# One expert tile normalised and stored a step, and TensorE two tiles ahead instead of one

## What is computed

```python
x = layernorm(x + attention(x))      # x: 4 x 1024 tokens of 128; 16 heads, 32 random features a head
# attention: q, k, v = x @ w_qkv;  elu1 features of q and k;  linear attention;  @ w_out + b_out
scores = x @ wr + br                 # router, 8 experts, the best one for each token
h = gelu(x @ w1[e] + b1[e])          # 128 -> 512, e the token's expert
y = h @ w2[e] + b2[e]                # 512 -> 128
out = layernorm(x + y)
```

## Time and profile before

| what | us |
|---|---|
| median of 3 runs (216.15 to 216.47) | 216.17 |
| span of the profiled execution, first to last instruction | 241.8 |
| PE busy in that span | 203.7 |
| DVE, ACT, POOL busy | 158.7, 146.5, 126.4 |

### The profile page before, as it was taken

The page is one execution under the profiler, slowest core; times in us unless marked ns, Lnnn a source line. Parts: engine busy times, 40 slices in busy tenths (PEclk is TensorE's granted clock), DMA queues, the critical chain, the costliest instruction groups (busy, mean ns, idle before and its releaser), DMA issues.

```text
span 241.8 us, 5983 instructions
## 1 busy us (share of the span) xinstructions
PE 203.7 (84%) x1717; PEld 160.5 (66%) x1717; DVE 158.7 (66%) x563; ACT 146.5 (61%) x379; POOL 126.4 (52%) x162
## 2 busy tenths in 40 slices
PE   7989999999999999998888359994997886999800
PEld 2768888888645555544357358993996875999700
DVE  1577686876669999999967226772664463467640
ACT  3488888888576887766275326662474453565810
POOL 8334252525971086665736761078553844577470
PEclk9999999999999999999999959999799998899965
DMA  4999999999710000012763334665564564461000
GB/s 114 246 395 409 412 409 411 412 408 321 225 52 0 5 34 34 34 36 54 237 163 117 94 101 114 169 188 157 144 178 130 164 186 138 134 184 45 11 28 0
DMA packets 28416, 40.45 MB, mean 167 GB/s; under 512 B 3497, under 2 KB 18126, under 8 KB 28384
## 3 DMA queue, kind: packets, MB, share of 16 engines
q1 hardware_dynamic: 26112, 35.80, 45.5%
q0 software_dynamic: 2272, 4.27, 5.2%
HBM read 17.95 MB, written 22.56 MB: 168 GB/s over the span
## 4 chain that ended last, share of the span: by engine, by line
PE 49%; issue 13%; POOL 11%; another core or an unknown queue 10%; ACT 8%; DVE 4%; DMA 1%; ACTq 1%; POOLq 1%; DVEq 0%
PE pair L312 13%; PE pair L792 13%; PE pair L805 7%; POOL sorted_rows L533 6%; PE bank L645 5%; ACT qfeat L964 3%; PE pair L785 2%; POOL rstd L514 2%; POOL out_dram L552 2%; PE bank L805 2%; PE pair L615 1%; PE bank L625 1%; ACT x L932 1%; DMA wqkv_sb<-in_L_attn_w_qkv_dram 1%
## 5 line engine op out<-in xcount | busy, mean ns | idle before, releaser
L964 ACT ACTIVATE qfeat<-pair,w_sb 128x128 f32<-128x128 f32 x156 | 44.6, 368 | 30.3 <-PE pair L792 17.5
L792 PE MATMUL pair<-xsT,w_slot 128*128 128x128 f32 x312 | 44.9, 290 | 4.3 <-ACT xsT L954 2.6
L792 PEld LDWEIGHTS pair<-xsT,w_slot 128*128 128x128 f32 x312 | 40.2, 202 | 6.7 <-issue 3.3
L533 POOL DMA_INDIRECT sorted_rows<-x,dest x32 | 31.6, 986 | 12.4 <-issue 8.8
L312 PE MATMUL pair<-wkv_part,xT_all 128*128 128x256 f32 x192 | 33.9, 321 | 1.1 <-ACT vals L886 0.8
L805 PE MATMUL pair<-w_sb,qfeat 128*128 x232 | 33.1, 289 | 0.7 <-issue 0.7
L561 POOL TENSOR_TENSOR ksum<-kfeat 128x512 f32<-128x512 f32 x12 | 16.6, 1379 | 30.7 <-DVE kfeat L1049 30.7
L805 PEld LDWEIGHTS pair<-w_sb,qfeat 128*128 128x128 f32 x232 | 30.6, 205 | 1.2 <-issue 1.1
L312 PEld LDWEIGHTS pair<-wkv_part,xT_all 128*128 128x128 f32 x192 | 28.4, 188 | 4.5 <-issue 4.4
L552 POOL DMA_INDIRECT out_dram<-x_all x26 | 26.2, 1009 | 9.3 <-issue 6.3
L312 PE MATMUL pair<-xT_all,wq_part 128*128 128x512 f32 x72 | 24.3, 457 | 0.0
(11 more groups left out here) (195 smaller groups left out, 406.1 us busy)
## 6 DMA issues: line engine op xcount, KB each, us to landing
sorted_rows<-pad_rows SPq DMA_DIRECT2D x11, 1584.0 KB, 22.5
w_slot<-in_L_ffn_w_dram SPq DMA_DIRECT2D x39, 256.0 KB
x_all<-in_L_attn_x_dram SPq DMA_DIRECT2D x8, 256.0 KB, 5.0
w_sb<-in_L_ffn_w_dram SPq DMA_DIRECT2D x4, 512.0 KB, 13.7
x_all<-sorted_rows SPq DMA_DIRECT2D x26, 66.0 KB
xs<-sorted_rows SPq DMA_DIRECT2D x13, 66.0 KB
w_sb<-in_L_ffn_b_dram SPq DMA_DIRECT2D x1, 512.0 KB, 7.5
sorted_rows<-x,dest POOLq DMA_INDIRECT x32
```

The lines of the kernel that those rows point to most:

```text
L533: g_.indirect_dma_start(out=sorted_rows, out_offset=bass.IndirectOffsetOnAxis(ap=dest[:, ring, i:i + 1], axis=0), in_=x1[:, ring, i, :], i ...
L792: last = mm(h_bank[t % 2][:, k * P:(k + 1) * P], w1_slot[:, t % WB, k * P:(k + 1) * P], xsT[:, t % 2, :], start=True, stop=True)
L964: a_.activation(hT[:, t % 2, k * P:(k + 1) * P], h_bank[t % 2][:, k * P:(k + 1) * P], ACT.Gelu, bias=w2_sb[:, bass.ds(w_at[t] + (FF + D + ...
```

## The change

The change has two parts. First, PE and ACT run two tiles ahead: in step s PE does turn(s+3), up(s+2), down(s), and ACT keep_rows(s+3), gelu(s+2). `xsT` and `hT` have three buffers instead of two, and the first products go round three banks from tile 4 on (bank 7 is the new one; up(4) waits until DVE has read the last ranks out of it). Secondly, DVE normalises one tile a step from step 5 on (two in steps 24 and 32), and POOL stores the tiles in order, with the power of batch j ahead of the tile that `POWER_BEFORE` names. The batches, the section after the loop, the loads and the number of every kind of instruction stay.

```diff
-        xsT = sb("xsT", [P, 2, P])
+        xsT = sb("xsT", [P, 3, P])
...
-        hT = qfeat[:, 0, 2:4, :]
+        hT = qfeat[:, 0, 1:4, :]
...
-        xs_bank, h_bank, y_bank = bank[0], [bank[1], bank[2]], [bank[3], bank[6], bank[4], bank[5]]
+        xs_bank, h_bank, y_bank = bank[0], [bank[1], bank[2], bank[7]], [bank[3], bank[6], bank[4], bank[5]]
...
-        NORMALISED_IN = {8: 0, 10: 1, 13: 2, 16: 3, 20: 4, 23: 5, 26: 6, 29: 7, 31: 8, 33: 9}
-        STORED_FIRST = (2, 3, 3, 3, 3, 3, 3, 2, 1, 2, 3)
+        BATCH_OF = {t: j for j, tiles in enumerate(BATCHES) for t in tiles}
+        NORMALISED_IN = {s: (s - 5,) for s in range(5, 24)}
+        NORMALISED_IN |= {24: (19, 20), 25: (21,), 26: (22,), 27: (23,), 28: (24,), 29: (25,), 30: (26,), 31: (27,), 32: (28, 29),
+                          33: (30,), 34: (31,), 35: (32,)}
+        POWER_BEFORE = {2: 1, 6: 2, 10: 3, 14: 4, 17: 5, 21: 6, 24: 7, 26: 8, 28: 9, 32: 10}
+        def hid(t):
+            return h_bank[t % 2] if t < 4 else h_bank[(t - 2) % 3]
...
-            for j, tiles in enumerate(BATCHES):
-                half = STORED_FIRST[j]
-                for t in tiles[0:half]:
-                    store(t)
-                if j + 1 < len(BATCHES):
-                    inverse_deviations(j + 1)
-                for t in tiles[half:]:
-                    store(t)
-            for t in range(ALONE, NT):
+            for t in range(NT):
+                if t in POWER_BEFORE:
+                    inverse_deviations(POWER_BEFORE[t])
                 store(t)
...
-                reach(pe, hT_ready, FC * (t - 1))
+                reach(pe, hT_ready, FC * (t - 1 if t < 4 else t - 2))
+                if t == 4:
+                    pe.wait_ge(row_ready, G)
+                    pe.wait_ge(next_ready, G)
...
             def tile_step(s):
+                if s + 3 < NT:
+                    turn(s + 3)
+                    weights_of(s + 3)
                 if s + 2 < NT:
-                    turn(s + 2)
-                    weights_of(s + 2)
-                if s + 1 < NT:
-                    up(s + 1)
+                    up(s + 2)
                 down(s)
...
             up(1)
             turn(2)
             weights_of(2)
-            down(0)
             ranks(G - 2)
             up(2)
             turn(3)
             weights_of(3)
-            down(1)
+            down(0)
             ranks(G - 1)
-            up(3)
-            turn(4)
-            weights_of(4)
-            down(2)
-            for s in range(3, NT):
+            for s in range(1, NT):
                 tile_step(s)
...
-                reach(act, hid_pre, t - 1)
-                a_.copy(xsT[:, t % 2, :], xs_bank[:, 0:P]).then_inc(xsT_ready, 1)
+                reach(act, hid_pre, t - 2)
+                a_.copy(xsT[:, t % 3, :], xs_bank[:, 0:P]).then_inc(xsT_ready, 1)
...
-                reach(act, y_pre, t - 1)
+                reach(act, y_pre, t - 2)
...
             def normalise_tiles(s):
-                if s in NORMALISED_IN:
-                    for t in BATCHES[NORMALISED_IN[s]]:
-                        normalise_tile(t, NORMALISED_IN[s])
+                for t in NORMALISED_IN.get(s, ()):
+                    normalise_tile(t, BATCH_OF[t])
```

More of the change, by code:

```diff
@@ L357, in build @@
         LAST_OF = {tiles[-1]: j for j, tiles in enumerate(BATCHES)}
-        NORMALISED_IN = {8: 0, 10: 1, 13: 2, 16: 3, 20: 4, 23: 5, 26: 6, 29: 7, 31: 8, 33: 9}
-        STORED_FIRST = (2, 3, 3, 3, 3, 3, 3, 2, 1, 2, 3)
+        BATCH_OF = {t: j for j, tiles in enumerate(BATCHES) for t in tiles}
+        LAST_ROWS = len(BATCHES[-1])
+        NORMALISED_IN = {s: (s - 5,) for s in range(5, 24)}
+        NORMALISED_IN |= {24: (19, 20), 25: (21,), 26: (22,), 27: (23,), 28: (24,), 29: (25,), 30: (26,), 31: (27,), 32: (28, 29),
+                          33: (30,), 34: (31,), 35: (32,)}
+        POWER_BEFORE = {2: 1, 6: 2, 10: 3, 14: 4, 17: 5, 21: 6, 24: 7, 26: 8, 28: 9, 32: 10}
+        assert sorted(t for tiles in NORMALISED_IN.values() for t in tiles) == list(range(ALONE - LAST_ROWS))
+        assert all(LAST_OF[BATCHES[BATCH_OF[t]][-1]] == BATCH_OF[t] and BATCHES[BATCH_OF[t]][-1] < s
+                   for s, tiles in NORMALISED_IN.items() for t in tiles)
+        def hid(t):
+            return h_bank[t % 2] if t < 4 else h_bank[(t - 2) % 3]
         def row_slot(t):
@@ L789, in up @@
                 pe.wait_ge(w1_loaded[t % WB], 16 * (t // WB + 1))
-                reach(pe, hT_ready, FC * (t - 1))
+                reach(pe, hT_ready, FC * (t - 1 if t < 4 else t - 2))
+                if t == 4:
+                    pe.wait_ge(row_ready, G)
+                    pe.wait_ge(next_ready, G)
                 for k in range(FC):
-                    last = mm(h_bank[t % 2][:, k * P:(k + 1) * P], w1_slot[:, t % WB, k * P:(k + 1) * P], xsT[:, t % 2, :],
+                    last = mm(hid(t)[:, k * P:(k + 1) * P], w1_slot[:, t % WB, k * P:(k + 1) * P], xsT[:, t % 3, :],
                               start=True, stop=True)
@@ L804, in down @@
                     pe.wait_ge(hT_ready, FC * t + k + 1)
-                    last = mm(y_bank[t % 4][:, 0:D], hT[:, t % 2, k * P:(k + 1) * P],
+                    last = mm(y_bank[t % 4][:, 0:D], hT[:, t % 3, k * P:(k + 1) * P],
                               w2_sb[:, bass.ds(w_at[t] + k * D, D)], start=(k == 0), stop=(k == FC - 1))
@@ L960, in gelu @@
                     act.wait_ge(attn_pre, G)
-                reach(act, y_pre, t - 1)
+                reach(act, y_pre, t - 2)
                 act.wait_ge(hid_pre, t + 1)
                 for k in range(FC):
-                    a_.activation(hT[:, t % 2, k * P:(k + 1) * P], h_bank[t % 2][:, k * P:(k + 1) * P], ACT.Gelu,
+                    a_.activation(hT[:, t % 3, k * P:(k + 1) * P], hid(t)[:, k * P:(k + 1) * P], ACT.Gelu,
                                   bias=w2_sb[:, bass.ds(w_at[t] + (FF + D + k), 1)]).then_inc(hT_ready, 1)
             def tile_step(s):
+                if s + 3 < NT:
+                    keep_rows(s + 3)
                 if s + 2 < NT:
-                    keep_rows(s + 2)
-                if s + 1 < NT:
-                    gelu(s + 1)
+                    gelu(s + 2)
             for s in range(G):
@@ L988, in _ @@
             keep_rows(4)
-            for s in range(3, NT):
+            for s in range(2, NT):
                 tile_step(s)
```

## The result

| kernel | median of 4 runs, us | lowest to highest |
|---|---|---|
| before | 216.32 | 216.15 to 216.50 |
| changed | 218.55 | 218.36 to 218.75 |

The ratio is 1.0088, with a 95% interval of 1.0068 to 1.0107: slower by 1.5 to 2.3 us. The forecast was 219.0 (+2.85), in a range of 215.9 to 220.2.

The account below looks back on a forecast made before the run. The prediction took the timed kernel as bound by PE at 1.90 us a step, with a start waiting for ACT and a tail waiting for POOL. Terms 0 + 1.90 + 0 + 0.95 = +2.85 on 216.17 gave 219.0 us, range 215.9 to 220.2.

Parts of the forecast that it names:

- Some of it has to be taken out: Profiled span against timed runs: late-signal gaps of 25.8 us are taken off the 241.8 us execution, leaving 216.0.
- the room of 0.2 to 3.2 us: Timed runs of the old kernel: what they can hold of late-signal gaps or time around the span.
- 136.4 less 0 to 3.0: Old kernel's start: step 3 should begin at 136.4, not 141.74; up to 3.0 us of an earlier wait may also go.
- The lead in the steps, 0: Full steps of PE: no gap to fill, gain 0; gelu's slack grows from 0.4 to 2.3 us.
- The lead at the start, +1.90: Before the steps: turn(5) comes at the same time, behind layer_norm(7), but each down a whole step later, +1.90 us.
- One tile normalised a step, 0: DVE in the steps: same number of normalisations, now even, while PE did not wait before; gain 0.
- The bound of 0.06 us a store: POOL's stores beside DVE normalisations: each costs at most 0.06 us more, off the path but for the tail.
- The tail, +0.95: After tile 35's add: seven stores behind the last power, last at 10.58 not 9.63, +0.95 us; bounds 0 and 1.35 plus 0.2.
- same: Rival, chance 0.09: late signals are in timed runs too, and the lead hides nearly all the room; 216.2 us.
- The clock: Rival, chance 0.06: PE's gap before up(2) grows to about 2.1 us and the clock falls, +1.7, 220.7 us.
- Faster: Rival, chance 0.12: downs wait a little for their gelu every timed step, so the lead wins; 215.1 at 0.12 us.
- the long waits end at a turn: Argument against "same": long waits in the steps end at a turn, whose slack the lead does not raise.

Follow-up runs that it names:

- experiment 1: The kernel before, unchanged, profiled again and timed against itself: 245.19 us, ratio 1.0007.
- experiment 9: The kernel before without POOL's stores of tiles 1 to 37: 223.00 us, ratio 0.9071 to before.
- experiment 10: The kernel before with only the two-tile lead added, and the stores of tiles 1 to 37 left out: 223.57 us, ratio 0.9104 to before.
- experiment 6: The kernel before with only the two-tile lead added, TensorE falling back to one tile in step 33: 242.75 us, ratio 0.9981 to before.
- experiment 5: The changed kernel, unchanged, run again: 236.59 us, ratio 0.9731 to a before of 243.44.
- experiment 4: The changed kernel with its last tiles normalised earlier, six stores behind the last power: 238.8 us, ratio 0.9801 to before.
- experiment 3: The kernel before with only the new normalising and storing order, TensorE one tile ahead: 240.25 us, ratio 0.9832 to before.

## Why the prediction was right, step by step

**Which execution is timed.** "Some of it has to be taken out" was the right move, and the room of 0.2 to 3.2 us held: in the changed kernel's trace without late signals turn(5) is at 133.65, inside 136.4 less 0 to 3.0. Of that room 1.75 us is time around the span, if it is the same before, so at most 1.4 us was left for waits of the old kernel. The reason was half wrong. I laid the gaps to the profiled execution; experiment 1 shows them in timed runs. The forecast holds for executions like those first timed, and only there. For the others its sign is wrong: -2.7%.

**The lead in the steps, 0.** Right: 1.90 us a step with one tile and with two (experiments 9 and 10). In the changed kernel gelu(5) ends at 138.59 and its down starts at 140.89, 2.3 us of slack as forecast.

**The lead at the start, +1.90.** Half shown. A fixed tile's add comes one step later after its turn in experiment 10 and in the changed kernel. The other half, that turn(5) comes at the same time in both kernels, no trace shows, and its reason was wrong: in the changed kernel gelu(3), and with it turn(5), waits for up(3) and not for layer_norm(7). The new order puts turn(4) ahead of up(3), which could make turn(5) up to 0.4 us later than in the old kernel (an estimate from that trace: up(3) starts at 130.74, and ranks(7) is done at 130.33). So the term may be too small, while the sum below is already too large: that the total came within 0.6 us owes something to luck. Before experiment 6 I split the step in 0.89 for the lost place of down(0) and 1.0 at the end; the run gave 1.9 back at the end, with intervals too wide to decide.

**One tile normalised a step, 0.** PE is full without gaps, so DVE's order costs nothing there. The bound of 0.06 us a store was too low: beside a normalisation the changed kernel's stores take up to 1.10 us against 0.98.

**The tail, +0.95.** It measured 10.78 - 9.63 = +1.15, inside its bounds; POOL was later by 0.27 us and not by 0.16, and the first two stores behind the power took 0.05 us more each. The 9.63 comes from traces with late signals.

**The sum.** 1.90 + 1.15 = 3.05 us, and the runs gave 2.2, in an interval of 1.5 to 2.3. So some 0.8 to 1.5 us are gained somewhere that no trace shows, since there is none of the kernel before without late signals. Short waits of the old kernel in its timed runs, which the lead takes away, would do it, and the room of 1.4 us would nearly hold them; that is the rival "same" in a small dose. It stays open.

**The rivals.** The clock did not fall: it is full up to the tail (1.00 from 137.99 to 198.80), and PE's gap ahead of up(2) is 0.95 us, not the 2.1 of that rival. "Faster" did not happen in the timed runs of the result, but in experiment 5. I had argued that the long waits end at a turn, which has no more slack than before, so that late signals would hurt both kernels alike. The table shows the lead alone doing little for them, 1 to 2 us, which agrees. What I did not ask is what makes signals late. The trace had a hint: PE was full from 146 to 158, where POOL was busy for 1.06 us, and had 10 us of gaps in the stretch where POOL was busy for 43.

## What to carry to other kernels

When an engine is full, a deeper lead on it gains nothing and is paid at its ends: count how many of its instructions stood in free time before, and what now stands ahead of the first result that the tail waits for. When a span and the timed runs differ by a tenth, find out what the extra time goes with before setting it aside; it can be the usual case in the next series of runs. Small stores issued in bursts can be worth spreading even where they seem hidden: here that took 4 us off in executions with late signals. Where there are none it gained nothing in the steps and lengthened the tail by 1.15 us, so leave fewer stores for the end (experiment 4's tail was 0.9 us shorter than experiment 3's).

## What was not expected of the hardware

TensorE's signals came late in the traces of all twelve experiments, on chips where the unchanged kernel took 243 to 246 us: up to 5 us in the steps (171.19 against a turn that ends at 166.21 in experiment 1), and up to 9 us beside the scatters (gelu(3) at 143.54 against an up(3) that ends at 134.17 in experiment 9). DVE and ACT often see them within 0.1 us of each other, 0.7 to 1.1 us after the last of three to five indirect DMAs in a row. The trace of the changed kernel's first runs (218.4 to 218.8) has none. Leaving out 37 indirect DMAs of POOL took 22 us off (0.9105), and writing 30 tiles by plain DMAs of ACT with one indirect DMA left gave the same, 0.9106. Storing one tile a step instead of up to five in a row took 4 us off.
